# Probability-times-V products of a layer kernel: two products with the same stationary tile made one of 129 columns

## What is computed

```python
qkv = jnp.einsum('bse,ehd->bshd', x, qkv_w) + qkv_b
q, k, v = jnp.split(qkv, 3, axis=-1)
logits = jnp.einsum('bqhd,bkhd->bhqk', q, k)
logits = logits / jnp.sqrt(jnp.asarray(q.shape[-1], logits.dtype))
logits = jnp.where(mask, logits, _large_negative_number(logits.dtype))
probs = jax.nn.softmax(logits, axis=-1)
attn = jnp.einsum('bhqk,bkhd->bqhd', probs, v)
...
x = x + _L0_attn_ref(_layernorm(x, axis=-1), ...)
x = x + _L0_ffn_ref(_layernorm(x, axis=-1), ...)
```

## Time and profile before

| | us |
|---|---|
| median of 3 runs | 967.18 |
| lowest, highest | 966.95, 969.72 |
| profiled execution | 963.67 |
| its span, first to last instruction | 961.9 |
| PE busy | 911.3 (95%) |
| POOL busy | 725.0 (75%) |
| DVE busy | 716.3 (74%) |
| ACT busy | 705.0 (73%) |

### The profile page before, as it was taken

How to read it: one execution, slowest core, us unless ns; L and a number is a source line. 1 busy time by engine, 2 the same in 40 slices (tenths; PEclk the granted TensorE clock), 3 DMA queues, 4 the chain that set the end, 5 groups by cost and what they waited for, 6 DMA issues and landing times.

```text
span 961.9 us, 25882 instructions
## 1 busy us (share of the span) xinstructions
PE 911.3 (95%) x10266; PEld 756.8 (79%) x10266; DVE 716.3 (74%) x1791; ACT 705.0 (73%) x889; POOL 725.0 (75%) x456
## 2 busy tenths in 40 slices
PE   4899999999999999999999999999999888769997
PEld 3567888888888888888888888888888675449996
DVE  7797878797869786878797879787978356437665
ACT  4456888888888888788878897888788963125562
POOL 1566888988898888888988898889788967154442
PEclk9799999999999999999999999999999999779999
DMA  6130435444444445444532331324030306112214
GB/s 197 42 89 2 96 80 120 84 108 86 115 97 108 88 117 105 100 95 114 98 80 65 82 83 55 87 59 105 2 89 2 142 1 267 37 42 62 62 45 139
DMA packets 71910, 82.95 MB, mean 86 GB/s; under 512 B 8928, under 2 KB 56162, under 8 KB 69616
## 3 DMA queue, kind: packets, MB, share of 16 engines
q1 hardware_dynamic: 69520, 77.08, 32.9%
q0 software_dynamic: 2272, 4.22, 1.2%
HBM read 22.84 MB, written 25.20 MB: 50 GB/s over the span
## 4 chain that ended last, share of the span: by engine, by line
PE 85%; DVE 8%; issue 3%; ACT 2%; DMA 1%; SPq 0%; POOL 0%; POOLq 0%; DVEq 0%; ACTq 0%
PE bg L1280 14%; PE st L1355 13%; PE st L1356 12%; PE pv L1387 7%; PE pv L1389 7%; PE pv L1391 6%; PE bg L1270 3%; PE bg L1245 3%; PE bg L1246 2%; PE bg L1247 2%; DVE row_max L1073 2%; PE bg L1529 2%; PE bg L1290 2%; PE st L1368 2%; PE bg L1520 1%
## 5 line engine op out<-in xcount | busy, mean ns | idle before, releaser
L620 POOL TENSOR_TENSOR p_lo<-prob,p_hi 128x1024 f16<-128x1024 f32 x320 | 617.1, 1946 | 120.0 <-ACT p_hi L758 118.7
L757 ACT ACTIVATE prob<-st,p_bias 128x1024 f32<-128x1024 f32 x320 | 329.6, 1030 | 132.6 <-PE st L1356 96.8
L758 ACT ACTIVATE p_hi<-st,p_bias 128x1024 f16<-128x1024 f32 x320 | 327.7, 1024 | 0.0
L1073 DVE TENSOR_REDUCE row_max<-bg 128x1 f32<-128x512 f32 x384 | 255.2, 685 | 17.1 <-PE bg L1280 11.7
L1355 PE MATMUL st<-big 128*128 128x512 f32 (+3 forms) x640 | 241.9, 380 | 2.4 <-ACT p_hi L758 2.4
L1280 PE MATMUL bg<-big 128*128 128x512 f32 (+3 forms) x640 | 232.3, 390 | 4.6 <-DVE big L1054 1.4
L1387 PE MATMUL pv<-v_parts,p_hi 128*128 128x65 f16 x2176 | 235.1, 194 | 1.4 <-POOL p_lo L620 1.4
L1387 PEld LDWEIGHTS pv<-v_parts,p_hi 128*128 128x128 f16 x2176 | 200.1, 96 | 44.4 <-issue 31.2
L1389 PE MATMUL pv<-v_parts,p_hi 128*128 128x64 f16 x2176 | 233.8, 195 | 0.0
L1356 PE MATMUL st<-big 65*128 65x512 f32 (+3 forms) x640 | 232.3, 368 | 0.0
L1391 PE MATMUL pv<-v_parts,p_lo 128*128 128x65 f16 x2176 | 232.2, 192 | 0.0
(11 more groups left out here) (233 smaller groups left out, 1158.0 us busy)
## 6 DMA issues: line engine op xcount, KB each, us to landing
big<-big SPq DMA_DIRECT2D x192, 128.0 KB, 2.3
row_dram<-fill SPq DMA_DIRECT2D x8, 1290.0 KB, 10.0
big<-part_dram SPq DMA_DIRECT2D x8, 1088.0 KB, 7.3
big<-big SPq DMA_DIRECT2D x16, 512.0 KB, 4.3
part_dram<-stage_parts SPq DMA_DIRECT2D x32, 176.0 KB, 3.1
part_dram<-stage_parts SPq DMA_DIRECT2D x16, 192.0 KB, 2.8
stage_raw<-ffn_w SPq DMA_DIRECT2D x16, 176.0 KB, 3.3
v_parts<-row_dram SPq DMA_DIRECT2D x39, 64.5 KB
```

The costliest lines, as they stand in the source:

```text
L620: nc.gpsimd.tensor_tensor(o, a, b, ALU.subtract).then_inc(p_lo_ready, 1)
L757: nc.scalar.activation(o32, src, ACT.Exp, bias=p_bias[:], scale=D ** -0.5)
L758: nc.scalar.activation(o16, src, ACT.Exp, bias=p_bias[:], scale=D ** -0.5).then_inc(exp_done, 1)
L1073: nc.vector.tensor_reduce(row_max[:, t, c:c + 1], bank, AX_X, ALU.max).then_inc(bg_drained, 1)
```

## The change

For query tiles 1 to 3 the two products of `p_hi` become one of 129 columns: V high, ones and V low side by side in `pv` (`pv_wide`, 3 x 129 columns), where the V-low part has 64 columns of its own. Tile 0 keeps its three products (`pv_first`, 65 columns), since four wide tiles don't fit into a bank of 512. The third product stays. DVE has to join the two sums: `normalise` copies the V-low part of the three wide tiles to `attn` (192 columns), takes the reciprocals, adds the V-high part from `pv` to `attn`, normalises tile 0 from `pv` with the reciprocal as a per-partition scalar, and multiplies the 192 columns in `attn` with their reciprocals, from SBUF to SBUF.

```diff
-        pv4 = pv[:, 0:4 * (D + 1)].rearrange("p (j c) -> p j c", c=D + 1)
+        pv_wide = pv[:, 0:3 * VW].rearrange("p (j c) -> p j c", c=VW)
+        pv_first = pv[:, 3 * VW:3 * VW + D + 1]
+        pv_sums = pv[:, D:3 * VW + D + 1:VW]
...
                 dve.wait_ge(p_used, h * NG + n + 1)
-                nc.vector.reciprocal(rden[:, B % 2], pv4[:, :, D:D + 1]).then_inc(rden_ready, 1)
+                head = slice(s * D, (s + 1) * D)
+                later = attn[:, 4 * b + 1:4 * b + 4, head]
+                nc.vector.tensor_copy(later, pv_wide[:, :, D + 1:VW])
+                nc.vector.reciprocal(rden[:, B % 2, :, 0], pv_sums).then_inc(rden_ready, 1)
                 dve.wait_ge(rden_ready, B + 1)
-                nc.vector.tensor_tensor(attn[:, 4 * b:4 * b + 4, s * D:(s + 1) * D], pv4[:, :, 0:D],
-                                        rden[:, B % 2].broadcast_to([P, 4, D]), ALU.mult).then_inc(attn_ready, 1)
+                nc.vector.tensor_tensor(later, later, pv_wide[:, :, 0:D], ALU.add).then_inc(pv_summed, 1)
+                nc.vector.tensor_scalar(attn[:, 4 * b, head], pv_first[:, 0:D], rden[:, B % 2, 3], None, ALU.mult)
+                dve.wait_ge(pv_summed, B + 1)
+                nc.vector.tensor_tensor(later, later, rden[:, B % 2, 0:3].broadcast_to([P, 3, D]), ALU.mult
+                                        ).then_inc(attn_ready, 1)
...
                 for j in range(max(0, kt - 4 * b), 4):
-                    out = pv4[:, j, :]
                     cols = slice(k * BLK + j * P, k * BLK + (j + 1) * P)
-                    nc.tensor.matmul(out, p_hi[:, n % PRING, cols], v[:, 0:D + 1],
-                                     start=(kt == 0 and j == 0), stop=False, skip_group_check=True)
-                    nc.tensor.matmul(out[:, 0:D], p_hi[:, n % PRING, cols], v[:, D + 1:VW],
-                                     start=False, stop=False, skip_group_check=True)
+                    high = p_hi[:, n % PRING, cols]
+                    out = pv_wide[:, j - 1, 0:D + 1] if j else pv_first
+                    if j:
+                        nc.tensor.matmul(pv_wide[:, j - 1, :], high, v, start=False, stop=False, skip_group_check=True)
+                    else:
+                        nc.tensor.matmul(out, high, v[:, 0:D + 1], start=(kt == 0), stop=False, skip_group_check=True)
+                        nc.tensor.matmul(out[:, 0:D], high, v[:, D + 1:VW], start=False, stop=False, skip_group_check=True)
                     mm = nc.tensor.matmul(out, p_lo[:, n % PRING, cols], v[:, 0:D + 1],
                                           start=False, stop=(kt == 4 * b + j), skip_group_check=True)
```

More of the change, by code:

```diff
@@ L348, in layer_kernel @@
         p_used, rden_ready, attn_ready = sem("p_used"), sem("rden_ready"), sem("attn_ready")
+        pv_summed = sem("pv_summed")
         bg_ready, bg_drained = sem("bg_ready"), sem("bg_drained")
```

## The result

| | median us | lowest, highest | ratio to before, 95% interval |
|---|---|---|---|
| before | 967.48 | 966.95, 969.72 | |
| after | 992.78 | 990.48, 994.43 | 1.0279 (1.0248 to 1.0310) |

The change makes the kernel 25.3 us slower, where 982.4 had been forecast, 15 us slower, in a range of 969 to 1012. The direction and the mechanism hold; the cost was ten microseconds larger than the sum said.

The account below looks back on a forecast made before the run. PE was taken to bound the kernel. Stalls of 21.2 us less a saving of 6.0 gave net +15.2 us, from the median of 967.18 to 982.4 us, in a range of 969 to 1012.

Parts of the forecast that it names:

- the sum: Whole kernel: stalls 21.2 us, of which 18.2 in heads 1 to 14, less 6.0 saved on PE, net +15.2 us.
- What bounds the kernel: In the attention PE bounds; a nanosecond less there is gained unless PE then waits, chiefly for DVE to empty pv.
- What PE saves: 1728 sets lose one product but no column: 3.5 ns each, 6.0 us, bounds 0 and 18.1.
- the rival in which it costs more than two narrow ones: At the wide products on PE: 81 ns each, 35 us more instead of -6, time 1023; chance 0.04.
- the one in which 10.5 ns a set are saved: PE's sets are paced by weight loads: 18.1 us saved meets 18 to 21 of stalls, 967 to 970; chance 0.09.
- What DVE is given: In normalise at block ends: 1.30 us against 0.64, so attn_ready comes 0.66 us later, bounds 0.50 and 0.85.
- Where that lands: PE's first product of a block waits at pv for 0.66 us less DVE's lead: 2.25 us for two heads.
- The term of 1 us for DVE's delay that outlives the stall: At background tasks whose bank was drained just in time, DVE's remaining delay costs 1 us together.
- Two SBUF inputs: DVE's last product is held by POOL in block 0 of even heads, 0.35 us more: 2.60 us for two heads.
- the rival: Last product misses POOL's gap and is held 2.15 us: time 1041 for 28 blocks, 1012 for 14; chance 0.21.
- The ends: First and last head: DVE further ahead, last normalise on the output path (0.66), some products held; 2 us together.

Follow-up runs that it names:

- The padded pair: Two more tile 0 products ahead of the last product, once in the kernel after (1099.11 us), once in the kernel with the sum joined in PSUM (1011.29 us).
- two kernels with the same wait: The kernel before with DVE's longer normalise alone (995.83 us), and the kernel after with the sum joined in PSUM (983.74 us).

## Why the prediction was right, and where it was small

**What bounds the kernel**: right. PE paid for every wait at `pv`, and the saving came through where the join was left out (ratio 0.9944).

**What PE saves**: right in kind. A full group, from its first product to the next instruction, in the kernel after:

```profile
414.03 0.19 PE L1400 MATMUL pv<-v_parts,p_hi 128*128 128x65 f16 x1
...
414.12 0.22 PE L1398 MATMUL pv<-v_parts,p_hi 128*128 128x129 f16 x1
414.18 0.19 PE L1402 MATMUL pv<-v_parts,p_lo 128*128 128x65 f16 x1
414.21 0.22 PE L1398 MATMUL pv<-v_parts,p_hi 128*128 128x129 f16 x1
...
414.74 0.42 PE L1289 MATMUL bg<-big 128*128 128x384 f32 x1
```

0.71 us where 0.73 stood, as for 3.5 ns a product; the medians over all full groups are 716 and 742 ns, 4.3 ns a wide set, 7.5 us for 1728, against 6.0 forecast. The wide product takes 55 to 63 ns to the next start, so the rival in which it costs more than two narrow ones falls, and so does the one in which 10.5 ns a set are saved.

**What DVE is given**: right, 1.29 us against 1.30, with all four durations within 6 ns.

**Where that lands**: right in place, small in size. I took PE to wait only for what exceeds the distance between the end of DVE's product and PE's start. But where PE does wait, it starts 0.056 to 0.058 us after DVE's end, never less; after the change this is the distance in 50 of the 64 block ends. The stall is therefore 0.66 less the distance plus 0.057. For two heads the steps at `pv` are 0.66 + 0.39 + 0.32 + 0.08 and 0.73 + 0.40 + 0.41 + 0.08, 3.07 us, with a further one of 0.13; forecast were 2.60, and the saving takes part of each step. Heads 1 to 14 lost 15.7 us net where the sum gives 18.2 less their share of the saving, 5.3, which is 12.9. The term of 1 us for DVE's delay that outlives the stall was about right: the step at group 15 comes in seven heads, 0.10 to 0.13 us each.

**Two SBUF inputs**: right, and the terms nearly: in block 0 of even heads the product lasts 0.63 to 0.65 us where 0.35 + 0.35 had been reckoned, and the margins of 0.2 us in front of POOL held, so the rival did not come about. One place was overlooked: block 2 had been read in the odd head 5 alone, and in even heads the product is issued just before a POOL instruction ends and lasts 0.43 us. The padded pair shows that the rival was a real one: with the product 0.38 us later the time is 1099.

**The ends**: this is the step that failed. "2 us together" for the first and the last head and the tail were in fact 5.0 + 6.9 - 0.7, some 11 us net, or 4.6 + 6.9 in the two heads from the end of group 0 on. The text named held products there and gave them no working. There were four, of 1.0 to 2.2 us, and the trace of the kernel before holds them: reckoned place by place as for block 0, from each reciprocal's start and POOL's instructions, the method gives these same four and stalls of about 1.5 us in head 0 and 3.8 in the last. The rest is the term for the clock that the sum did not have. In head 0 the clock cost 1.1 us, by a fall that two kernels with the same wait don't show, so this part was not to be foreseen; in the last head it is at its lower level for 10.2 us instead of 3.4, and what that costs beside the waits was not separated. Joined in PSUM, the two heads lose 4.0 us instead of 11.4.

## What to carry to other kernels

A product saved on the bounding engine is worth what a product costs beyond its columns, here 4.3 ns; a partner's work between two uses of a single PSUM bank is worth its whole length less the lead that the partner had. Write that lead down for every such place, also in the first and the last round of the loop, which had the largest surprises here, before giving the partner more to do. Where VectorE works beside GpSimd, keep one input of each VectorE product of two tensors in PSUM if it can be had. And when a loss is read from two traces, first see how far they differ where the change can't reach: here by up to 3.1 us.

## What the runs showed of the hardware

- A VectorE product of two SBUF tensors that is issued while GpSimd subtracts two SBUF tensors ends 0.21 to 0.22 us after GpSimd's instruction does: up to 2.15 us instead of 0.35 in the kernel after. With one input in PSUM none of 64 was held (344 to 348 ns). The Trainium skill (SBUF — State Buffer, section Who interferes with whom) says that a VectorE instruction with two SBUF inputs contends with a GpSimd instruction that reads SBUF, and that one with at most one such input, outside the two-port modes, does not. The traces agree. That whoever issues first has the ports for its whole instruction it says of the two-port modes; the held rows show the same for this product of two tensors.
- In the kernel after, PE's first product of a block, where it waited for VectorE's last product, starts 0.056 to 0.058 us after that product's end (50 places).
- fp16 products of 65 columns, each with its own weight load, start 29 ns apart (median), those of 129 columns are followed after 55 to 63 ns.
- GpSimd takes 0.51 us for the product of 192 columns that takes VectorE 0.35.
- After a wait of 1.57 us near the start of the first head PE's granted clock was 0.50 for 3.4 us; in two other kernels, after 1.57 and 1.56 us at the same place, it stayed at 1.00. So the length of that one wait does not tell whether the clock falls.
